# Second edge pass of a graph network: the queue that moves the node rows goes from ACT to SyncE

## The reference, cut to what matters

```
h   = relu(layernorm(x))
x   = x + GCN(h)          # agg = segment_sum(norm * h[row], col); out = agg @ W.T + b; layernorm(out) * gamma + beta
h   = relu(layernorm(x))
x   = x + RGCN(h)         # uses h @ bases[b] for four bases b
```

## Time and profile before

| what | us |
|---|---|
| time before, median of 3 runs (10969.58 to 10983.56) | 10974.4 |
| span of the profiled execution, first to last instruction | 10879.4 |
| what lies around the span, by difference to the median | 95.0 |
| second edge pass in that span (2515 to 4985) | 2470 |

### The profile page before, as it was taken

How to read it: one execution, slowest core, us unless ns; L and a number is a source line. 1 busy time by engine, 2 the same in 40 slices (tenths; PEclk the granted TensorE clock), 3 DMA queues, 4 the chain that set the end, 5 groups by cost and what they waited for, 6 DMA issues and landing times. The chain is left out here.

```text
span 10879.4 us, 143542 instructions
## 1 busy us (share of the span) xinstructions
PE 7281.4 (67%) x34582; PEld 5619.6 (52%) x34582; DVE 4894.6 (45%) x12591; ACT 1925.5 (18%) x5149; POOL 6900.4 (63%) x6291
## 2 busy tenths in 40 slices
PE   2555555554666666668888888888836666666667
PEld 2444444443333333336777777777724555555555
DVE  5444444444665565654222222222264555555556
ACT  1111111111111111112222222222221111111111
POOL 3666666665666666665888888888815555555553
PEclk6555555555555555556777777777755555555555
DMA  6222222222222222223444444444472222222222
GB/s 236 56 56 58 57 56 58 55 57 59 74 71 74 75 71 76 71 75 66 56 56 55 56 56 56 55 56 56 53 212 67 68 68 65 67 66 67 65 66 52
DMA packets 809417, 765.69 MB, mean 70 GB/s; under 512 B 128472, under 2 KB 701362, under 8 KB 809073
## 3 DMA queue, kind: packets, MB, share of 16 engines
q0 software_dynamic: 375872, 414.65, 22.5%
q1 hardware_dynamic: 340391, 271.94, 8.2%
q10 hardware_dynamic: 92938, 77.03, 2.3%
HBM read 544.72 MB, written 224.78 MB: 71 GB/s over the span
## 5 line engine op out<-in xcount | busy, mean ns | idle before, releaser
L1412 POOL DMA_INDIRECT scat<-msg_out,msg_idx x1564 | 2414.3, 1544 | 491.5 <-issue 319.8
L2001 POOL DMA_INDIRECT soft_rows<-proj,soft_slot x1564 | 1487.5, 951 | 1385.1 <-DVE soft_x L2188 718.2
L721 POOL DMA_INDIRECT L_rows<-H,L_slot x1568 | 1493.2, 952 | 993.3 <-issue 596.3
L988 POOL DMA_INDIRECT L_rows<-H,L_slot x1568 | 1496.5, 954 | 890.4 <-issue 464.5
L1505 PE MATMUL msg_ps_msg<-msg_hb,msg_lhs 128*128 128x128 f32 x6272 | 1600.9, 436 | 1.2 <-DVE msg_lhs L1478 1.2
L1505 PEld LDWEIGHTS msg_ps_msg<-msg_hb,msg_lhs 128*128 128x128 f32 x6272 | 1493.0, 328 | 185.3 <-issue 183.9
L1478 DVE SCALAR_TENSOR_TENSOR msg_lhs<-msg_dst_sp,msg_node,msg_ps_c 128x512 f32<-128x512 f32 x784 | 551.2, 745 | 2040.4 <-ACT msg_dst_sp L1433 1813.0
L2130 PE MATMUL soft_ps_sum<-soft_onehot,soft_x 128*128 128x64 f32 x3136 | 752.8, 422 | 306.0 <-DVE sums_b L2247 216.9
L861 PE MATMUL L_sum<-L_onehot,L_rows 128*128 128x64 f32 x3136 | 691.0, 392 | 392.9 <-issue 337.6
L2130 PEld LDWEIGHTS soft_ps_sum<-soft_onehot,soft_x 128*128 128x128 f32 x3136 | 705.6, 328 | 371.3 <-issue 276.8
L861 PEld LDWEIGHTS L_sum<-L_onehot,L_rows 128*128 128x128 f32 x3136 | 657.9, 305 | 433.9 <-issue 423.6
(11 more groups left out here) (365 smaller groups left out, 10133.3 us busy)
## 6 DMA issues: line engine op xcount, KB each, us to landing
L_rows<-H,L_slot POOLq DMA_INDIRECT x3136
msg_hb<-HB SPq DMA_DIRECT2D x392, 128.0 KB
soft_at_in<-in_edge_attr_dram SPq DMA_DIRECT2D x195, 256.0 KB
scat<-L_zeros SPq DMA_DIRECT2D x64, 408.0 KB
rel_parts<-scat SPq DMA_DIRECT2D x100, 256.0 KB, 5.2
HB<-L_prod ACTq DMA_DIRECT2D x49, 512.0 KB
scat<-msg_out,msg_idx POOLq DMA_INDIRECT x1564
soft_rows<-proj,soft_slot POOLq DMA_INDIRECT x1564
```

The source lines that it names most:

```text
L721: pool.indirect_dma_start(rows[:, k, j, :], None, t["H0"], bass.IndirectOffsetOnAxis(ap=slot[:, k, j:j + 1], axis=0)).then_inc(gathered[k] ...
L988: pool.indirect_dma_start(rows[:, k, j, :], None, t["H1"], bass.IndirectOffsetOnAxis(ap=slot[:, k, j:j + 1], axis=0)).then_inc(gathered[k] ...
L1412: pool.indirect_dma_start(t["scat"][j], bass.IndirectOffsetOnAxis(ap=idx[:, k, j:j + 1], axis=0), out[:, k, j, :], None, compute_op=ALU.ad ...
L2001: pool.indirect_dma_start(rows[:, s % SC, j, :], None, t["proj"], bass.IndirectOffsetOnAxis(ap=slot[:, s, j:j + 1], axis=0)).then_inc(gath ...
```

## The change

The three functions `load_nodes`, `store_x` and `store_products` leave ACT's list and enter SP's. Their waits are the same, with an empty instruction behind each wait. The place of the load stays -1 (step 7, for the pair that is turned in the next body). `store_x` moves from place 7 to 8 and `store_products` from 15 to 16, that is from step 7 to step 0 of the next body, for the same pair. SP's list now has in step 0: `load_ids`, `store_x`, `store_products`; in step 4: `load_ids`; in step 7: `load_nodes`.

```diff
-            with_nodes(sp, S, t, [(0, load_ids)], [])
+            def load_nodes(m, groups):
+                sp.wait_ge(node_dv, m * C + 20)
+                sp.nop(nofuse=True)
+                sp.dma_start(h_n[:, :, :], tiles_of(t["H1"], m * 2, 2)).then_inc(h_in, 16)
+                sp.dma_start(x_n[:, :, :], tiles_of(t["X1"], m * 2, 2)).then_inc(h_in, 16)
+
+            def store_x(m, groups):
+                sp.wait_ge(node_dv, m * C + C + 18)
+                sp.nop(nofuse=True)
+                sp.dma_start(tiles_of(t["X2"], m * 2, 2), x2[:, :, :]).then_inc(x_out, 16)
+
+            def store_products(m, groups):
+                sp.wait_ge(finished, m * CF + 2 * CF)
+                sp.nop(nofuse=True)
+                sp.dma_start(tiles_of(t["HB"], m * 2, 2), prod[:, :, :]).then_inc(hb_out, 16)
+            with_nodes(sp, S, t, [(0, load_ids)], [(-1, load_nodes), (8, store_x), (16, store_products)])
...
-            def load_nodes(m, groups):
-                act.wait_ge(node_dv, m * C + 20)
-                act.dma_start(h_n[:, :, :], tiles_of(t["H1"], m * 2, 2)).then_inc(h_in, 16)
-                act.dma_start(x_n[:, :, :], tiles_of(t["X1"], m * 2, 2)).then_inc(h_in, 16)
-
-            def store_x(m, groups):
-                act.wait_ge(node_dv, m * C + C + 18)
-                act.dma_start(tiles_of(t["X2"], m * 2, 2), x2[:, :, :]).then_inc(x_out, 16)
-
-            def store_products(m, groups):
-                act.wait_ge(finished, m * CF + 2 * CF)
-                act.dma_start(tiles_of(t["HB"], m * 2, 2), prod[:, :, :]).then_inc(hb_out, 16)
...
             with_nodes(act, S, t, [(R, give_indices), (0, store_coefficients)],
-                       [(-1, load_nodes), (4, root_first), (7, root_second), (7, store_x), (9, normed), (11, copy_turned), (13, copy_first),
-                        (15, copy_second), (15, store_products)], after=after)
+                       [(4, root_first), (7, root_second), (9, normed), (11, copy_turned), (13, copy_first), (15, copy_second)], after=after)
```

## The result

The changed kernel takes 11007.04 us (median of 5, 10991.68 to 11014.72), the kernel before in the same comparison 10970.08 us (10955.82 to 10983.56): ratio 1.003, 95% interval 1.0019 to 1.0040, or +37 us. The prediction said 11020 us, slower by 46.

What follows compares the result with a forecast made beforehand. No engine was full; the ring PE multiply, ACT slot, POOL gather was taken as the bound. Lateness 2.4 less relief 1.15, at eight tenths 1.0 us over 45 bodies, plus 1 at the end: 11020 us, range 10945 to 11085.

Steps and rivals of the forecast that it cites:

- The relief: Second edge pass, step 0: ACT's slot comes earlier without four issues of step 7, 1.15 us a body.
- share of eight tenths: Estimated part of the net lateness on the ring that reaches the body: 1.0 of 1.25 us.
- lower bound of 0.6 us a body: Low side of the gain at step 0's slot, from POOL's own stop: 1.16 us in one body form, nothing in the other.
- The lateness: Step 7: types and ids queued on SP behind the node loads reach PE 2.4 us late a body on average.
- second form of body: About half of the bodies, where norm ends inside a stretch of slow SP issues; ids put 2.7 us late.
- 95.0 us around the span: Time outside the profiled span, taken as unchanged and added to the span of 10925 us to give 11020.
- The end of the pass: IDX is stored behind the last HB store in SP's order, delaying the next phase by 1 us, once.
- All is absorbed: Rival: POOL waits about 8.8 us a body whatever happens and the two slips cancel; 10974 us, chance 0.27.
- The relief wins: Rival: ids arrive in time or inside a stall, ACT's slots come 1.15 us earlier; 10951 us, chance 0.22.
- No absorption: Rival: ids 2.8 us late, gain only 0.5 us, so +2.3 us a body; 11080 us, chance 0.12.
- rule of the rings: Descriptors of a ring go in order, so ids stand behind 256 KB of node rows: estimated 0.6 us, 27 in the sum.
- hold: Stretch of unknown cause in a body: ACT idle 8.40 us, SP issues 1.84 us apart instead of 0.46.

Runs made afterwards that it cites:

- ids-first kernel: Changed kernel with load_nodes one place later in SP's list, behind load_ids of the next step 0; 0.9988 and 0.9981 of the kernel before in two comparisons.
- C: Comparison on another chip than the other two, four kernels timed in turns with the kernel before, which took 10998.87 us; changed kernel 1.0028.
- later wait: Kernel before, plus a transfer-free wait in SP's step 7 for the constants of the second norm (DVE, step 6); 11132.98 us, 1.0124.
- A: Comparison timing four edited kernels in turns with the kernel before, which took 10895.62 us; the changed kernel was not in it.
- wait alone: Kernel before, plus a wait for norm with no transfer in SP's step 7; 1.0000 and 1.0001 of the kernel before in two comparisons.
- B: Comparison timing the changed kernel and three others in turns with the kernel before, which took 10988.26 us; changed kernel 1.0027.
- loads alone: Kernel before with only load_nodes moved to SP, both stores staying on ACT; 0.9999 and 1.0029 of the kernel before in two comparisons.

## Why the prediction was right

**The mechanism.** SP's `load_ids` behind the node loads makes the ids late, PE's L1184 waits, the slot of step 7 and POOL follow: shown, by the ids-first kernel in C (the same transfers on the same queues, 51 us less), by the later wait (no transfer moved to another queue, +145 us), and by POOL's stop of step 7, which grows by 3.5 us while the others together shrink. The step is right.

**The relief.** The slot of step 0 should come 2.1 us behind its product: 2.09 in the body above, and in the median of the changed kernel. Its worth is the ids-first kernel against before: 20 us in C (0.19%, interval 0.10 to 0.28%), 11 us in A. The sum had 1.15 x 0.8 x 45 = 41 us, two to four times too much. The two bodies that the term was read from (3.54 and 4.35 us from product to slot) stand for the pass only in part: the mean over 44 bodies of the kernel before is 4.69 us, and with ACT's issues gone and the ids first it is still 3.63 in A, so much of the delay has another cause. What the issues took is 1.06 us of it at A's pace, and 0.87 in C (6.12 with the wait alone, 5.25), near the 1.15 reckoned. But POOL's stop behind it shrinks only by 0.2 us at A's pace (1.51 before, 1.29) and by 0.5 in C (2.95 and 2.42); 45 bodies of that are 10 and 24 us, near the 11 and 20 timed. These are single traces, in which other stops shift by as much. Too large, it seems, was the share of eight tenths. The lower bound of 0.6 us a body, which would have given 22 us, was close by luck: it came from two bodies, and POOL's mean stop at that place was 1.51 us.

**The lateness.** Foreseen were 2.4 us a body, of which eight tenths arrive, 86 us. Measured: PE waits about 5 us a body for them; its stop at this place is 4.5 us longer than with the ids first (6.47 and 2.00), and about a quarter of that arrives, 51 us. Two errors of opposite sign. In the second form of body I let the types go at about +5.7 and had PE stopped 2.7 us by it; in the body above they go at +7.38 and PE stops 8.70. Counted through the timeline of the changed kernel, in the 43 bodies behind the first three and ahead of the last three, the types leave more than 4 us behind `norm` in 24, so "about half" was right and its size too small. Where I failed is the list of what SP does between `norm` and the types: in the body above not only its issues are slow but the loop turn and the register work of the waits too, three instructions of 0.70 us each (3142.63, 3144.06 and 3145.48), each with about as much behind it.

**The share that arrives.** 0.8 was a guess for both signs. The runs show no constant share: about nothing of the wait for `norm`, a quarter of what the changed kernel adds to PE's stop, two thirds in the longest wait (4.5 us of PE, 3.0 of the time). The gain is smaller than its sum for the same reason: POOL waits for slots some three times a body, about 3 us each, and the others can take up a part of what one of them gains or loses.

**The sum.** +46 us foreseen; +37, +28 and +30 us measured in three comparisons. The right total came from two terms that were each about twice too large (51 instead of 86, 20 instead of 41), so it is luck. In both the share of eight tenths was too large; in the lateness the size, 2.4 us for 4.5, was too small beside it.

**"95.0 us around the span"** was no such thing. The profiled run of the changed kernel took 10991.68 us with a span of 10989.9: 1.8 us lie around it. The trace of before looks like that of an execution at the quicker pace: its span, 10879.4, and its first pass, 2357.4, are as in A (10896 us; 2358 to 2362), while the median was of a slower one. The error stood on both sides of the difference and did no harm.

**What would show it.** L1186 and L1110 wait for `id_rows` or `types` by DMA: 29 times in 36 bodies; said were 45 in the pass, or 33 in as many. POOL's waits for slots: 342.3 / 36.1 = 9.5 us a body, said 9.8. The body: 49.88 us in the first trace of the changed kernel, said 49.7, but in C the fair pair is 2457.1 / 48.97 = 50.2 for the changed kernel and 49.4 for that with the wait alone, whose time is that of before: +0.7, said +1.0. The end of the pass:

```profile
5057.84 0.37 SPq L984 DMA_DIRECT2D HB<-L_prod  x1
5058.27 0.46 SPq L987 DMA_DIRECT2D IDX<-L_idx  x1
5063.09 0.37 ACTq L1425 DMA_DIRECT2D msg_idx_all<-IDX  x1
```

The next phase begins 5.25 us behind the last `HB` store, 3.25 before: 2 us, said 1.

**The rivals.** *All is absorbed* fell in B and C for the changed kernel, but it describes the wait alone (2 us a body, 1.000 twice) and the loads alone at A's pace (0.9999). The rule of the Trainium skill (DMA: Bandwidth & Descriptors, "Issuing engines are not separate DMA queues"), that only a sequencer's issue time is saved, agrees with the ids-first kernel: the saving is real and small, 11 to 20 us of 11,000 for four issues a body. The loss comes from something beside that rule, the order inside a queue with waits. *The relief wins* needed ids that aren't late; the ids-first kernel is that rival made true, 20 us below before in C and 11 in A, where it said 23. *No absorption* had +2.3 us a body; about 0.6 to 0.7 was measured.

The same page's rule of the rings (the Trainium skill, "Queues, rings and completion order") would make the ids land later behind the node rows; the prediction put 27 us on it (22 by its own eight tenths). The traces don't put the cost there, and don't settle the rule. Where PE waited for the ids, it started behind the issue of its types by a median of 2.8 us in the changed kernel in C and 3.2 with only the loads on SP, both with 256 KB just ahead in SP's queue, and by 3.5 with the wait for `norm` and 2.6 with the later wait, with none. (In A it is 3.7 with the loads and 2.8 with the wait, and both are free.) What differs in C is when the types are issued: a median of 0.9 us behind `norm` with the wait alone, 4.2 with the two loads between. So the loads cost there by the time that SP takes to get past them, as far as its records in holds can be trusted.

**What stays open.** Why the loads alone cost nothing in A and 31 us in C. In A's trace the types leave more than 4 us behind `norm` in 5 of 43 bodies, in C's in 23, counted as above. It is not simply that at A's pace `norm` ends outside a hold: with the wait alone it is the other way round, 21 of 43 in A and 6 in C, and that kernel costs nothing in either. Why the pace differs, also in code that no edit touches, and what a hold is, no run here tells. The changed kernel was not timed at A's pace.

## What to carry to other kernels

A transfer that is moved to another engine brings its wait along: before moving it, write down the new queue in order and ask of each entry behind the wait when it used to be issued. Here one place in a list (the ids ahead of the node loads, which then wait alone at the queue's end) turns a loss of 0.3% into a gain of 0.2%, with the same transfers, of which only the ids leave at another moment. The gain was 0.1% at A's pace, where the changed kernel was not timed. When such a lateness is sized, ask first how much the other stops can give back, and take a larger dose of it as an experiment: the first gave 0, the second 145 us. And read a term from many bodies, not from two.

## What the runs showed of the hardware

The same kernel before took 10896, 10988 and 10999 us in A, B and C (10970 beside the first result), up to 0.9% apart, while its runs inside each lie within 0.33%. A and B ran on one chip, so it is not the chip alone, and TensorE's mean granted clock is 0.58 in all. The untouched first pass has two paces as well, 2358 to 2362 us in A and 2383 to 2386 in B and C, and the third pass (L1412 before the change, L1414 behind it) has not (2887.9 to 2889.7 in all). An edit's worth differed between them: 1.0029 against 0.9999 for the same kernel.

Inside a hold many of SP's sequencer instructions stand at 0.70 us each in the records, the issues among them (L966, 3147.61 in the body above). It is not the transfers that are slow there (the types were in use 3.4 us behind their issue) but the way to the issue: from the second node load to the types 5.7 us pass in the body above, against the 0.9 us reckoned for a body without a hold. From `norm` to the types the median is 5.7 us in that trace and 2.15 in that of only the loads on SP in A.
